# A selective scan in units of two states by 64 channels, with one product in four on GpSimd

## The reference

```
x_in = concat(x_norm, x_norm[:, ::-1])                 # two directions: 8 sequences
xr, z = split(x_in @ W_in); xr = silu(conv4(xr))       # 192 channels e, 4 taps
dbl = xr @ W_xproj                                     # 6 for dt, 16 B, 16 C
dt = softplus(dbl[:6] @ W_dt + b_dt)
h[e,n] = exp(dt[e] * A[e,n]) * h[e,n] + dt[e]*x[e]*B[n]  # scan along L, 16 states n
y[e] = sum_n h[e,n] * C[n] + D[e]*xr[e];  out = (y * silu(z)) @ W_out
```

## Time and profile before

| | us |
|---|---|
| runs (3): median, lowest, highest | 1229.33, 1225.15, 1230.13 |
| the profiled execution, its span | 1225.61, 1223.7 |
| first layer's loop, first scan to end of the last | 56.6 to 771.6 |
| second layer | from 781.9 |

### The profile page before, as it was taken

How to read it: one execution, slowest core, us unless ns; L and a number is a source line. 1 busy time by engine, 2 the same in 40 slices (tenths; PEclk the granted TensorE clock), 3 DMA queues, 4 the chain that set the end, 5 groups by cost and what they waited for, 6 DMA issues and landing times. The chain is left out here.

```text
span 1223.7 us, 9473 instructions
## 1 busy us (share of the span) xinstructions
PE 1078.3 (88%) x3294; PEld 369.1 (30%) x3294; DVE 964.5 (79%) x635; ACT 549.0 (45%) x574; POOL 878.0 (72%) x348
## 2 busy tenths in 40 slices
PE   7789999889988999989978878599999999996675
PEld 2233333333232333324322222223333333332221
DVE  1499999899998999999989999600296796969771
ACT  5755857796657464756573634111111020110321
POOL 0079799888878778978988966400098969789890
PEclk9879999899999989998988989879999999998787
DMA  2144355434354434453434444163849595682502
GB/s 78 71 141 151 140 157 137 156 123 153 121 157 123 153 122 138 136 173 126 170 121 138 133 144 136 25 153 76 129 102 188 84 204 83 141 133 39 107 1 73
DMA packets 106863, 150.95 MB, mean 123 GB/s; under 512 B 62818, under 2 KB 75848, under 8 KB 106816
## 3 DMA queue, kind: packets, MB, share of 16 engines
q1 hardware_dynamic: 104832, 143.65, 44.7%
q10 hardware_dynamic: 1984, 6.70, 2.0%
HBM read 123.27 MB, written 10.70 MB: 109 GB/s over the span
## 5 line engine op out<-in xcount | busy, mean ns | idle before, releaser
L690 POOL TENSOR_TENSOR hc<-h,c_rep 128x1024 f32<-128x1024 f32 x192 | 451.2, 2358 | 175.7 <-DVE h L734 169.5
L734 DVE TENSOR_TENSOR_SCAN h<-a,bu 128x1024 f32<-128x1024 f32 x192 | 439.0, 2286 | 20.1 <-ACT a L564 2.4
L390 PE MATMUL y_ps<-hc,ident 128*128 128x512 f32 x768 | 384.7, 625 | 2.9 <-POOL hc L690 1.7
L564 ACT ACTIVATE a<-dt,a_neg 128x1024 f32<-128x1024 f32 x192 | 218.6, 1148 | 224.5 <-DVE h L734 216.6
L724 DVE TENSOR_TENSOR bu<-bu,u 128x1024 f32<-128x1024 f32 x192 | 232.1, 1209 | 16.2 <-PE bu L369 16.2
L1147 POOL TENSOR_TENSOR prod_p<-vw,at 128x3584 f32<-128x3584 f32 x18 | 130.2, 7235 | 124.2 <-DMA vw<-v_d 120.8
L390 PEld LDWEIGHTS y_ps<-hc,ident 128*128 128x128 f32 x768 | 145.3, 197 | 213.3 <-issue 188.7
L1028 PE MATMUL sc_ps<-x,w_up 128*64 128x512 f32 x672 | 177.6, 604 | 0.0
L1028 PE MATMUL sc_ps<-x,w_low 96*64 96x512 f32 x672 | 177.3, 603 | 0.0
L369 PE MATMUL bu<-st,pick 96*64 96x512 bf16 (+1 forms) x512 | 120.2, 394 | 47.0 <-DVE h L734 41.3
L1098 ACT ACTIVATE sc<-sc_ps,rel 128x512 f32<-128x512 f32 x24 | 16.6, 690 | 248.4 <-PE sc_ps L1028 248.4
(11 more groups left out here) (124 smaller groups left out, 928.3 us busy)
## 6 DMA issues: line engine op xcount, KB each, us to landing
c_rep<-c_d SPq DMA_DIRECT2D x128, 512.0 KB, 3.6
c_rep<-c_d SPq DMA_DIRECT2D x128, 256.0 KB, 3.9
vw<-v_d SPq DMA_DIRECT2D x24, 532.0 KB, 9.6
x<-qk SPq DMA_DIRECT2D x66, 171.0 KB, 6.4
scores_d<-sc ACTq DMA_DIRECT2D x24, 196.0 KB
at<-scores_d SPq DMA_DIRECT2D x24, 196.0 KB, 4.7
x<-qk SPq DMA_DIRECT2D x22, 152.0 KB, 6.7
v_d<-v SPq DMA_DIRECT2D x4, 541.5 KB, 6.2
```

What stands on the lines that cost most here:

```text
L390: mm = pe.matmul(y_ps[:, cols(th)], ident[:, :], hc[:, k % HC_RING, cols(th)], start=(n == 0 and d == 0), stop=(n == N_ST - 1))
L564: nc.scalar.activation(a[:, k % A_RING, :], dt[:, tile % 2, :], ACT.Exp, scale=a_neg[:, kind_of(tile), n:n + 1]).then_inc(exp_done, 1)
L690: nc.gpsimd.tensor_tensor(hc[:, k % HC_RING, :], h[:, k % H_RING, :], c_rep[:, k % C_RING, :], ALU.mult).then_inc(hc_done, 1)
L734: nc.vector.tensor_tensor_scan(scan_order(h[:, k % H_RING, :], d), scan_order(a[:, k % A_RING, :], d), scan_order(bu[:, k % 2, :], d), 0.0 ...
```

## The change

- **Units.** Unit k of a tile is now two states (2m, 2m+1; m = n // 2) by 64 channels; the two halves of the rows hold the two states, and units alternate between the channel halves (`half`). There are 192 units as before. dt and u therefore exist twice a tile, each half of the channels copied to both halves of the rows by transfers on SP (six of 256 KB a tile; tile 0 has four on SP and two on ACT). Every c_rep load is two of 256 KB, for L tiles too, where it was one of 512 KB.
- **Sum.** `sum_states` adds a pair of units with `fold` (128x64): for each half of the positions two float32 matmuls of 64 columns, one to the upper and one to the lower 64 rows of y_ps; a loop does one half of the positions. It now stands ahead of `front`, and it waits for `hc_done` of both units. The skip term is a matmul with a diagonal `diag_d`.
- **B.** In each unit with k % 4 == 2 (48 of 192) SP broadcasts the two rows of B from DRAM into `b_rep` (ring of 2), GpSimd multiplies them by u three loops ahead, and TensorE copies the product into bu with the identity (two float32 matmuls in place of two bfloat16 ones); DVE only scans.
- **Front.** The splits of B (rest, low) and the sums of softplus (sum) are matmuls with the identity and its negative, in place of GpSimd's. conv and sum take four loops of two matmuls, xp, rest and low two loops, the others one. ACT empties both banks with one instruction (`leave_both`), and u is the only GpSimd instruction left of them. HC_RING is 5.
- **Start.** For tile 0 DVE makes the splits and the three sums before u; dt and u are then spread by transfers.

```diff
+POOL_UNITS = [k for k in range(N_TILES * N_ST) if k % 4 == 2]
+B_RING, B_AHEAD = 2, 3
+PLAN = [(0, "xp", 1, 0), (3, "dt", 1), (4, "rest", 1, 0), (7, "sum", 1), (9, "low", 1, 0), (11, "conv", 3), (15, "dt", 2), (16, "conv", 5),
...
# SP, loop k
+                for part in range(2):
+                    n = N_ST + 2 * m + part
+                    sp.dma_start(c_rep[E_HI * part:E_HI * part + E_HI, k % C_RING, :],
+                                 bc_d[2 * b + d, n:n + 1, :].to_broadcast([E_HI, L])).then_inc(c_in[k % C_RING], 16)
+                if k + 2 in POOL_UNITS and k + 2 > POOL_UNITS[0]:
+                    load_b(POOL_UNITS.index(k + 2))
+                    if since == 4:
+                        left(sp, J("sum", t_next, 1))
+                        second_half(dt, t_next, dt_b)
+                    if since == 6:
+                        sp.wait_ge(u_done, t_next + 2)
+                        sp.wait_ge(dt_b, 32 * (t_next + 1))
+                        first_half(dt, t_next, dt_a)
+                        second_half(u, t_next, u_b)
+                    if since == 7:
+                        sp.wait_ge(u_b, 32 * t_next + 16)
+                        first_half(u, t_next, u_a)
...
# TensorE, spread_b
+                if k in POOL_UNITS:
+                    pe.wait_ge(b_times_u, i + 1)
+                    mm = pe.matmul(bu[:, k % 2, cols(th)], ident[:, :], b_rep[:, i % B_RING, cols(th)], start=True,
...
# TensorE, sum_states
+                pe.wait_ge(hc_done, k + 2)
+                for half in range(2):
+                    rows = slice(E_HI * half, E_HI * half + E_HI)
+                    mm = pe.matmul(y_ps[rows, cols(th)], fold[:, :], hc[:, (k + half) % HC_RING, cols(th)],
...
             for k in range(UNITS):
                 spread_b(k + 1)
+                if k >= SUM_LAG:
+                    sum_states((k - SUM_LAG) // 2 * 2, (k - SUM_LAG) % 2)
                 front(k)
-                if k >= SUM_LAG:
-                    sum_states(k - SUM_LAG)
...
# GpSimd
+            for k in range(B_AHEAD):
+                b_product(k)
             for k in range(UNITS):
+                b_product(k + B_AHEAD)
                 read_out(k)
                 front(k)
...
# ACT, before its loop
+            act.wait_ge(u_done, 2)
+            act.dma_start(u[E_HI:128, 0, 0, :], u[0:E_HI, 0, 0, :]).then_inc(u_a, 16)
+            act.dma_start(u[0:E_HI, 0, 1, :], u[E_HI:128, 0, 1, :]).then_inc(u_b, 16)
...
# DVE
             for k in range(UNITS):
-                times_b(k)
+                if k not in POOL_UNITS:
+                    times_b(k)
                 scan(k)
```

More of the change, by code:

```diff
@@ L67 @@
 PLAN = [
[4 rows of a table removed]
[L72 to L76, removed]
@@ L85 @@
-LAST = [("out", 5, 3, 0), ("out", 5, 3, 1)]
-JOBS = [f + (th,) for f in FIRST for th in range(2)] + [p[1:] for p in PLAN] + LAST
-DONE_AT = {p[1:]: p[0] + STEPS.get(p[1], 1) for p in PLAN}
+    (0, "xp", 1, 0), (3, "dt", 1), (4, "rest", 1, 0), (7, "sum", 1), (9, "low", 1, 0), (11, "conv", 3), (15, "dt", 2),
+    (16, "conv", 5), (20, "sum", 2), (24, "xp", 0, 1), (26, "z", 0), (27, "rest", 0, 1), (30, "dt", 3),
+    (31, "low", 0, 1), (33, "cen", 2), (34, "sum", 3), (38, "conv", 4), (42, "var", 2), (44, "xp", 1, 1),
@@ new lines @@
+    (46, "cen", 3), (47, "dt", 4), (48, "rest", 1, 1), (50, "var", 3), (51, "sum", 4), (55, "low", 1, 1),
+    (57, "conv", 6), (61, "conv", 7), (65, "dt", 5), (66, "xp", 2, 0), (69, "sum", 5), (73, "rest", 2, 0),
+    (75, "z", 1), (76, "out", 0, 0), (78, "dt", 6), (79, "low", 2, 0), (82, "sum", 6), (86, "conv", 8), (90, "z", 2),
+    (91, "out", 1, 1), (92, "xp", 3, 0), (95, "dt", 7), (96, "rest", 3, 0), (99, "sum", 7), (103, "low", 3, 0),
+    (105, "conv", 9), (110, "dt", 8), (111, "out", 2, 0), (112, "out", 2, 1), (114, "sum", 8), (118, "conv", 10),
@@ new lines, with steps @@
+    (122, "xp", 2, 1), (125, "z", 3), (126, "dt", 9), (127, "rest", 2, 1), (130, "sum", 9), (134, "low", 2, 1),
+    (136, "conv", 11), (140, "xp", 3, 1), (143, "dt", 10), (144, "rest", 3, 1), (147, "sum", 10), (151, "low", 3, 1),
+    (158, "dt", 11), (162, "sum", 11), (168, "z", 4), (169, "out", 3, 2), (184, "z", 5), (186, "out", 4, 2),
+    (187, "out", 4, 3)]
+LAST = [("out", 5, 3)]
+JOBS = [j + (th,) for j in FIRST + [p[1:] for p in PLAN] + LAST for th in range(2)]
+def steps(name, *job):
+    if name in ("conv", "sum"):
+        return 2 if job == (1,) else 4
+    return 2 if name in ("xp", "rest", "low") else 1
@@ new lines, in low_job @@
+            def low_job(b, d, th):
+                rows = slice(0, 2 * N_ST)
+                out = bank("low", b, d, th)[rows, :]
+                free(J("low", b, d, th))
+                left(pe, J("rest", b, d, 1))
+                pe.matmul(out, ident[rows, rows], dbc[rows, b % 2, cols(th)], start=True, stop=False)
+                pe.matmul(out, minus_i[rows, rows], st[rows, seq_slot(b, d), cols(th)], start=False, stop=False)
+                pe.matmul(out, minus_i[rows, rows], mid[rows, cols(th)], start=False,
+                          stop=True).then_inc(job_done, 1)
@@ L359, in spread_b @@
                     return
[L360 to L363 removed]
+                tile, m, half, seq = unit(k)
+                if k in POOL_UNITS:
+                    i = POOL_UNITS.index(k)
+                    pe.wait_ge(b_times_u, i + 1)
+                elif k % N_ST < 2:
+                    if seq == (0, 0):
+                        pe.wait_ge(split_first, 4)
+                    else:
+                        left(pe, J("low", *seq, 1))
                 if k >= 2:
@@ L432, in leave, with leave_both @@
                 nc.scalar.activation(out, src, func, **kw).then_inc(left_act, 1)
+            def leave_both(job, out, rows, func=ACT.Identity, **kw):
+                act.wait_ge(job_done, J(*job, 1))
+                nc.scalar.activation(out, banks(rows), func, **kw).then_inc(left_act, 2)
             def xi(b, s):
@@ new lines, in rest_left, with low_left, natural @@
+            def rest_left(b, d):
+                act.wait_ge(job_done, J("rest", b, d, 1))
+                nc.scalar.activation(st[64:96, seq_slot(b, d), :], banks(slice(64, 96)), ACT.Copy)
+                nc.scalar.activation(mid[0:32, :], banks(slice(0, 32)), ACT.Copy).then_inc(left_act, 2)
+            def low_left(b, d):
+                leave_both(("low", b, d), st[0:32, seq_slot(b, d), :], slice(0, 32), ACT.Copy)
+            def natural(tile):
+                return 1 if tile == 0 else tile % 2
@@ L780, in _ @@
             for _, *job in LAST:
-                add_out(*job)
+                for th in range(2):
+                    add_out(*job, th)
             left(dve, len(JOBS))
```

523 lines of the change are left out of this document (282 added, 241 removed), and 7 rows, old and new, of the table PLAN.

## The result

The changed kernel takes 1291.72 us (median of 4 runs, 1289.42 to 1292.97) against 1228.18 of the kernel before on the same chip: a ratio of 1.0518, 95% interval 1.0489 to 1.0546. It is 5% slower; the forecast was 1214, its range ended at 1244. The profiled span is 1290.2 us, 66.5 more than before. The stage (the first layer's loop) runs from 61.94 to 835.4 us: 773.5 against 715 before and 699 forecast, and 5.3 of the rest is its later start.

The account below looks back on a forecast made before the run. DVE was taken as the bound, TensorE close behind. After the change the stage was 673 + 18 + 3 + 5 = 699 us against 715; with +3.7 for start and end, 1225.6 - 16 + 3.7 = 1213, given as 1214, range 1184 to 1244.

Parts of the forecast that it names:

- Start: Ahead of the first layer's loop: copying u across the halves puts the first scan at about 61.5 us, +5 us.
- Prices of TensorE: Start-to-start times of TensorE's matmuls in a loop: spread 0.52, two full float32 matmuls 1.82, 64-column pair 1.01 us.
- TensorE becomes the bound of tiles 0 to 8: Loops 0 to 143: TensorE has 514 us of work, 57.1 a tile, against DVE's 458.
- TensorE's granted clock [...] 5 us, ends 0 and 10: Added wait in the stage: 1.2 GHz behind the longer wait for u, with more TensorE work in the first loops.
- Two us a tile [...] 18: Added waits in nine tiles: TensorE waits for ACT to empty both banks; 18 us, ends 0 and 36.
- 3 for `hc_done`: Added wait in the stage: GpSimd's passes for u or B delay hc and so the sum; 3 us, ends 0 and 20.
- the thin part: Loops 144 to 191, with few front pieces: TensorE 130 us, DVE 159 with gates and additions, no waits added.
- The chain of B: Third rival: late landings of B delay GpSimd, hc and sums; 48 us over the stage without waits, total 1244; chance 0.18.
- the bare stage: First layer's loop without waits: 514 us for loops 0 to 143 plus 159 for the rest, 673 against 715.
- Nothing changes: Second rival: bank hand-overs cost their upper end, 36 in place of 18; stage 717, total 1231; chance 0.16.
- DVE bound: First rival: DVE stays the bound or nearly, TensorE's waits vanish in idle loops; stage 673, total 1187; chance 0.17.
- The sums on TensorE (36 x 1.82 = 66 us): Softplus' sums among TensorE's front pieces in loops 0 to 143: 36 pieces at 1.82, 66 us.

Follow-up runs that it names:

- e13: Changed kernel with zero matmuls ahead of the sum in fifteen loops, sized to TensorE's stands (98 in all, 22.5 us): 1278.63 us.
- e1: Changed kernel without B's 96 transfers; GpSimd multiplies u by u, so B is left out of one unit in four: 1282.05 us.
- e7: Changed kernel with B loaded four units ahead in place of two, and SP's wait for u's copy one loop later: 1281.80 us.
- e6: Changed kernel with the bfloat16 spread written four times in place of once in the 44 loops without front work: 1294.90 us.
- e10: Changed kernel with three of the four terms of softplus' sum on TensorE left out, so the sum is incomplete: 1266.70 us.
- e5: Changed kernel with ACT emptying the two banks of a dt job in one pass in place of two: 1288.19 us.
- e11: Changed kernel with ACT's silu put behind softplus at three boundaries (loops 16, 66, 111), where it stood ahead of dt's evacuation: 1295.90 us.
- e16: Changed kernel with conv and softplus' sum in two pieces of four matmuls in place of four of two: 1308.33 us.
- e9: Changed kernel with twelve zero matmuls added to the open sum of y ahead of the job behind each dt job: 1287.52 us.
- e3: Changed kernel with C and B each loaded in one transfer of 512 KB to 128 partitions in place of two of 256 KB: 3017.32 us.
- e14: Changed kernel with DVE emptying dt's banks behind its scan in tiles 1 to 11, ACT then reading SBUF: 1292.51 us.

## Why the prediction was wrong

**Right.** Start: 5.3 us later, first scan at 61.94 (forecast +5, 61.5). Prices of TensorE: a full loop 3.35, with a spread of B 4.65, a fold pair 0.9 to 1.0 (priced 1.01). TensorE becomes the bound of tiles 0 to 8, and DVE stands for the spread there. GpSimd's work is 586 us (592). The rows of C and B move 186 GB/s at a share of 0.79 (205 and 0.76).

**Wrong: the lower clock.** The step "TensorE's granted clock [...] 5 us, ends 0 and 10" looked only at the start. It is 46 us in tiles 0 to 8 alone (e13's account above). The earlier trace rows had the hint in 0.95 for the whole stage: some 72 us at the lower level. What they cost while DVE was the bound no run shows; DVE stood only 14.9 us for its spreads there. I had read it off one stretch at the start. The forecast made TensorE the bound and should have priced that clock from then on: a tenth of the time at half speed is 5% of 514, or 26 us, with no new fall at all. Of the 74.5 us that the loop is over the forecast (773.5 against 699), 41 are this term.

**Wrong in size: the stands.** "Two us a tile [...] 18" for banks is 22.8 in the trace, 3 for `hc_done` is 0.7, and some 6 us of waits for DVE were not priced; 29.6 in all against 21, so 8.6 over. Of the hand-overs 14.3 are where they were put: 11.1 behind dt's two passes and 3.2 behind a split of B held up by softplus. The others wait for silu, z, var and a convolution, and ACT's silu with its table loads (3.6 us) ahead of dt's passes was left out.

**Wrong: the thin part.** Tiles 9 to 11 take 184 us and not 159, which is the remaining 25. DVE is busy 155.6 of them, as forecast; the forecast put its waits there at nothing and gave no reason. It stands 28, of which 15 are scans behind a float32 spread and 6 products behind a bfloat16 one. B's transfers are 6 to 7 us of it (e1, e7). TensorE runs there at 0.87, but the clock is hardly the rest: e6 has 0.94 and 20 us of low in place of 48 in these tiles and takes 184.2 (with filler in its free loops). TensorE's spread waits for the scan by turns with DVE waiting for it; no run took that apart.

**The rivals.** The chain of B exists: landings of 5.3 us median, 79 us of waits on GpSimd. It was priced at 48 us over the bare stage and cost 10. "Nothing changes" and "DVE bound" needed less, not more, from TensorE. The sums on TensorE (36 x 1.82 = 66 us) are a cause of the loss against the kernel before, e10 gives 25 us back alone and 34 with the other two gone, but not of the miss: the forecast had them at their price. No rival held that TensorE's terms would run slower than priced, on an engine without slack.

**On the transfers** the changed kernel's windows say:
```profile
184.00:190.00 6.00, 5.33 (x14) 1.09 (x14) 5.13 (x4) 5.97 (x6) 1.11 (x2) 0.59 1.06 255
566.00:586.00 20.00, 17.64 (x47) 4.79 (x48) 17.13 (x10) 16.41 (x16) 14.15 (x7) 0.87 1.01 237
```
That is 255 GB/s in six us and 237 in twenty, in pairs of pieces to the two halves of the partitions. The Trainium skill has some 218 GB/s as the limit of a transfer that reaches one half (SBUF — State Buffer, "Door 1: The DMA port swizzle"), and next to nothing more from a second one to the other half (the same page, "Can I just issue two DMAs to hit both halves?"). Together the two are not borne out here, as they were not in the earlier trace rows before.

## What stays open

What it is in the dt job that lets the clock fall. A stand alone does it in some places (behind waits of 1.5 to 2.1 us in tiles 9 to 11), and the dt job without a stand does it in 53 places of the traces. In the kernel before, dt's two halves stood in separate loops, 1.07 us each with 128-row matmuls between, and the fall followed two or three of eleven within 4 us; the change put both halves into one loop. It fits e5, e11 and e16, which were to shorten stands and gained little or nothing, and e9 and e13, whose filler stood directly behind dt (in each only three of eleven dt jobs have a fall within 5 us). That the rows or the length of the job are the reason was not tried: the run that would tell is the changed kernel with dt's halves in two loops again, or with a dt matmul over all rows of `dbc`.

## What to carry to other kernels

Before a change moves the bound to TensorE, take the granted clock of the whole stage from the windows and charge TensorE's new sum with it; time at the lower level costs half its length wherever TensorE is the bound (106 us cost some 50 here). Then look at what stands in the queue of the engine that empties TensorE's banks at that moment, table loads included. When several causes share one loop, undoing one gives less than its price: here 10, 13 and 25 us alone (48) were 61 together. And before a cause is called a cause of the miss, look whether the forecast had it already.

## What was unexpected of the hardware

- A single transfer that spreads two rows of 4 KB over 64 partitions each (e3) brought the kernel to 3017 us. The DMA engines' share was 0.16 over long stretches with 58 GB/s, 0.13 with 52 in the quietest, which is the work of two or three of the 16; the packets were no smaller (3.9 KB on average from 200 to 1200 us, against 3.3 in the changed kernel from 200 to 800); two transfers of one row each (the changed kernel) moved 186 GB/s.
```profile
1000.00:1100.00 100.00, 26.49 (x64) 7.38 (x64) 19.71 (x12) 12.96 (x12) 25.57 (x11) 0.62 0.18 62
```
- TensorE's clock went to 1.2 GHz with the engine busy and no stand before it 53 times in 19 traces, each time 1.8 to 3.5 us behind the start of some 1.9 us of matmuls over 6 rows (e14: 1.93 us, busy 2.00 of 2.00).
